# Rounding without a grid, two homes for rounded rows, and the last tiles in smaller parts

## What is computed

```python
x = x + L0_ffn(L0_cond(x, fside, ...))      # attention, then experts: silu(h @ w1) * (h @ w3) @ w2
x = x + L1_ffn(L1_cond(x, fside, ...))

def reorder_quantize(x, idx):               # L1_ffn
    scale = max(abs(x)) / (448 * 6)
    xr = (x / scale)[:, idx]
    scale_x = max(abs(xr), axis=1) / 448    # one for each row
    return fp8_e4m3(xr / scale_x), scale_x, scale
g = quantised(x) @ quantised(w_gate)        # 256 -> 704
u = quantised(x) @ quantised(w_up)
t = silu(g) * u
y = quantised(t) @ quantised(w_down)        # 704 -> 256
```

## Time and profile before

| | us |
|---|---|
| median of 3 runs | 626.72 (625.84 to 627.07) |
| profiled execution | 625.02 |
| its span | 623.2 |
| mean granted clock of TensorE | 0.961 |

### The profile page before, as it was taken

One profiled execution on the slowest core, in us unless ns is written; L12 is line 12 of the kernel. 1 busy time (PEld: TensorE's weight loads), 2 busy tenths in 40 slices (PEclk: granted clock), 3 DMA queues, 4 the chain that ended last, 5 costly groups with the idle time before them and its releaser, 6 DMA issues.

```text
span 623.2 us, 10889 instructions
## 1 busy us (share of the span) xinstructions
PE 495.9 (80%) x3862; PEld 406.4 (65%) x3862; DVE 506.2 (81%) x981; ACT 361.1 (58%) x762; POOL 241.2 (39%) x204
## 2 busy tenths in 40 slices
PE   2011298599999999999748999999999999475774
PEld 1000143278888878888618999999999999332542
DVE  4999878688888888987354979989999899489993
ACT  3336235777787778876307457565555556356671
POOL 3244014744444445541436079642514420170011
PEclk9999999989999999999859999999999999888897
DMA  8300004050000000000149799889888753130001
GB/s 267 135 1 1 0 1 135 0 178 2 1 2 2 1 2 9 19 9 2 58 157 357 259 331 281 273 267 257 300 290 271 274 130 119 34 103 17 9 25 36
DMA packets 36530, 71.87 MB, mean 115 GB/s; under 512 B 5275, under 2 KB 21915, under 8 KB 36219
## 3 DMA queue, kind: packets, MB, share of 16 engines
q10 hardware_dynamic: 15280, 40.77, 19.6%
q1 hardware_dynamic: 18123, 22.26, 10.6%
q0 software_dynamic: 3072, 8.14, 5.2%
HBM read 66.03 MB, written 5.12 MB: 114 GB/s over the span
## 4 chain that ended last, share of the span: by engine, by line
PE 55%; DVE 27%; issue 7%; ACT 5%; DMA 3%; POOL 1%; SPq 1%; DVEq 0%; ACTq 0%; POOLq 0%; PEldq 0%
PE pw L437 9%; PE pb L437 9%; PE pt L631 6%; PE pb L631 6%; PE sc L478 6%; PE sc L631 6%; PE po L437 5%; PE pt L489 3%; DVE areg L1181 2%; DVE areg L1167 2%; DVE areg L1165 2%; DVE rs L1579 2%; DMA wreg<-in_L_ffn_w 1%; DVE breg L1238 1%; DVE areg L1614 1%
## 5 line engine op out<-in xcount | busy, mean ns | idle before, releaser
L1730 POOL TENSOR_TENSOR breg<-breg,con 128x512 f32<-128x512 f32 x32 | 40.7, 1272 | 81.4 <-ACT breg L864 81.4
L437 PE MATMUL pb<-areg,wreg 128*128 128x512 f16 x240 | 58.4, 379 | 2.1 <-ACT breg L864 1.9
L437 PE MATMUL pw<-areg 128*128 128x256 f16 x406 | 56.5, 273 | 2.7 <-DVE areg L1533 2.7
L872 ACT ACTIVATE breg<-breg,mx 128x128 f32<-128x128 f32 (+1 forms) x128 | 56.5, 444 | 2.0 <-DVE mx L1289 2.0
L478 PE MATMUL sc<-areg,breg 128*128 128x128 f32 (+1 forms) x256 | 48.6, 334 | 6.7 <-DVE mx L1289 5.5
L631 PE MATMUL pb<-areg,wreg 128*128 128x128 f32 x448 | 52.7, 275 | 0.6 <-ACT areg L965 0.6
L985 ACT CAST areg<-areg 128x512 f16<-128x512 f32 (+1 forms) x46 | 25.9, 563 | 46.8 <-DVE areg L1519 43.6
L631 PEld LDWEIGHTS pb<-areg,wreg 128*128 128x128 f32 x448 | 51.3, 192 | 0.9 <-issue 0.8
L631 PE MATMUL pt<-areg,wreg 128*128 128x128 f32 x424 | 49.9, 275 | 1.3 <-DMA wreg<-in_L_ffn_w 1.3
L631 PEld LDWEIGHTS pt<-areg,wreg 128*128 128x128 f32 x424 | 48.5, 192 | 1.5 <-DMA wreg<-in_L_ffn_w 1.4
L631 PE MATMUL sc<-areg,wreg 128*128 128x128 f32 x416 | 48.9, 275 | 0.0
(11 more groups left out here) (250 smaller groups left out, 1286.4 us busy)
## 6 DMA issues: line engine op xcount, KB each, us to landing
wreg<-in_L_ffn_w ACTq DMA_DIRECT2D x40, 896.0 KB, 8.1
wreg<-in_L_ffn_w SPq DMA_DIRECT2D x14, 896.0 KB, 8.3
ys_dram<-areg ACTq DMA_DIRECT2D x23, 128.0 KB
wreg<-in_L_ffn_wq SPq DMA_DIRECT2D x1, 2048.0 KB, 8.9
wreg<-in_L_ffn_wo SPq DMA_DIRECT2D x1, 2048.0 KB, 8.2
areg<-in_fside_BxSxS ACTq DMA_DIRECT2D x4, 256.0 KB, 5.4
x_in<-in_x SPq DMA_DIRECT2D x4, 256.0 KB, 3.9
h_dram<-areg SPq DMA_DIRECT2D x8, 128.0 KB, 1.7
```

The lines of the kernel that those rows point to most:

```text
L437: last = nc.tensor.matmul(bank, w(a), m(b), start=first and k == 0, stop=final and k == 2)
L872: last = nc.scalar.activation(pr[:, parity, b, o:o + w], pr[:, parity, b, o:o + w], ACT.Exp, bias=mx[:, parity, k:k + 1], scale=-1.0, accu ...
L1730: G.tensor_tensor(t2[:, parity, :].rearrange("p (b n) -> p b n", b=2), t2[:, parity, :].rearrange("p (b n) -> p b n", b=2), rope_sin.rearr ...
```

## The change

In `nearest_e4m3` the instruction that takes the exponent bits goes. ScalarE makes the raised value with `Abs` instead of `Copy` and a factor of 2**20 - 2**10 instead of 2**20, and VectorE adds and takes off that value itself. `scale_of_rows` takes the reciprocal of the peak first. `qt` gets a second home. The last row tile (7) is scaled, rounded, transposed and copied in two halves of 352, with its down product in `sc2`, between other TensorE work in a new order. The w2 of the last expert tile (22) is split at the end of iteration 21; the folds of layer 2 move behind it. Lines of a part that repeat its pattern are left out.

```diff
+RAISE = 2.0 ** 20 - 2.0 ** 10
-        qt = cut(areg, 4864, INTER // 2, F16)
+        qts = [cut(areg, at, INTER // 2, F16) for at in (4864, 14464)]
...
 # TensorE
+            def part_transposes(i, h, bank):
+                pe.wait_ge(s["qt_ready"], i + 1 + h)
+                for c in range(h * NI // 2, (h + 1) * NI // 2):
+                    last = nc.tensor.transpose(bank[0:IQ, :].bitcast(F16)[:, c * P:(c + 1) * P], qts[i % 2][:, c * IQ:(c + 1) * IQ], identb[:, :])
+                last.then_inc(s["qtT_done"], 1)
+            def part_products(i, h):
+                pe.wait_ge(s["qtT_copied"], i + 1 + h)
+                for c in range(h * NI // 2, (h + 1) * NI // 2):
+                    last = nc.tensor.matmul(sc2[:, 1, 0:D], qtT[i % 2][0:IQ, c, :], q1d[0:IQ, c, :], start=c == 0, stop=c == NI - 1)
+                if h == 1:
+                    last.then_inc(s["dn_done"], 1)
...
             inner_transposes(NT - 2)
             down_quantised(NT - 3)
-            keep_clock(pt2[:, 1, :], 3)
+            pe.wait_ge(s["inner_ready"], NT)
+            keep_clock(pb[0], 4)
+            pe.wait_ge(s["qtT_copied"], NT - 1)
+            part_transposes(NT - 1, 0, pt2[:, 0, :])
+            part_transposes(NT - 1, 1, pt2[:, 1, :])
             down_quantised(NT - 2)
-            inner_transposes(NT - 1)
-            keep_clock(pt2[:, 1, :], 4)
-            down_quantised(NT - 1)
+            part_products(NT - 1, 0)
+            part_products(NT - 1, 1)
...
 # ScalarE, expert loop
-                if n < MT:
+                if n < MT - 1:
                     w2_high(n, parity)
                     inner_high(n, parity, 0)
+                if n < MT:
                     act.wait_ge(s["upb_done"], n + 1)
...
+                    if n == MT - 1:
+                        inner_high(n, parity, 0)
                     inner_high(n, parity, 1)
...
-                if n in (20, 21):
-                    fold_high(n - 20)
+                if n == MT - 2:
+                    w2_high(MT - 1, 1 - parity)
+                if n >= MT - 1:
+                    fold_high(n - MT + 1)
...
 # ScalarE, second layer (the same in scaled_input)
-                nc.scalar.activation(traised[i % 2], tvals[i % 2], ACT.Copy, scale=rs[:, 9, i:i + 1]).then_inc(s["scaled_ready"], 1)
+                nc.scalar.activation(traised[i % 2], tvals[i % 2], ACT.Abs, scale=rs[:, 9, i:i + 1]).then_inc(s["scaled_ready"], 1)
+            def scaled_parts(i):
+                act.wait_ge(s["inv_ready"], i + 1)
+                act.wait_ge(s["qt_ready"], i - 1)
+                for h in range(2):
+                    at = slice(h * IH, (h + 1) * IH)
+                    nc.scalar.activation(tscaled[i % 2][:, at], tvals[i % 2][:, at], ACT.Copy, scale=rs[:, 8, i:i + 1])
+                    nc.scalar.activation(traised[i % 2][:, at], tvals[i % 2][:, at], ACT.Abs, scale=rs[:, 9, i:i + 1]).then_inc(s["scaled_ready"], 1)
...
 # VectorE, expert loop
-                w2_low(n, n % 2)
+                if n < MT - 1:
+                    w2_low(n, n % 2)
                 inner_low(n, n % 2, 1)
...
-                if n >= MT - 2:
-                    fold_low(n - MT + 2)
+                if n == MT - 2:
+                    w2_low(MT - 1, (MT - 1) % 2)
+            for m in range(2):
+                fold_low(m)
...
 # VectorE, second layer
-                link(V.tensor_scalar(out, peak, 1.0 / FP8_MAX, None, ALU.mult))
-                link(V.reciprocal(inverse, out))
-                V.tensor_scalar(raised, inverse, 2.0 ** 20, None, ALU.mult).then_inc(done, 1)
+                link(V.reciprocal(turned, peak))
+                V.tensor_scalar(inverse, turned, FP8_MAX, None, ALU.mult)
+                V.tensor_scalar(raised, turned, FP8_MAX * RAISE, None, ALU.mult).then_inc(done, 1)
+                return V.tensor_scalar(out, peak, step, None, ALU.mult)
...
-                link(V.tensor_scalar(g.bitcast(I32), raised.bitcast(I32), 0x7F800000, 0x00400000, ALU.bitwise_and, ALU.bitwise_or))
-                link(V.scalar_tensor_tensor(v, g, FP8_LEAST * MAGIC, v, ALU.max, ALU.add))
-                return V.scalar_tensor_tensor(dst, g, FP8_LEAST * MAGIC, v, ALU.max, ALU.subtract, reverse1=True)
+                link(V.scalar_tensor_tensor(v, raised, FP8_LEAST * MAGIC, v, ALU.max, ALU.add))
+                return V.scalar_tensor_tensor(dst, raised, FP8_LEAST * MAGIC, v, ALU.max, ALU.subtract, reverse1=True)
...
             def round_inner(i):
                 dve.wait_ge(s["scaled_ready"], i + 1)
-                if i >= 1:
-                    dve.wait_ge(s["qtT_done"], i)
+                if i >= 2:
+                    dve.wait_ge(s["qtT_done"], i - 1)
...
-            round_inner(NT - 1)
+            round_parts(NT - 1)
```

More of the change, by code:

```diff
@@ L709, in inner_transposes @@
                 for c in range(NI):
-                    last = nc.tensor.transpose(pt2[0:IQ, 0, :].bitcast(F16)[:, c * P:(c + 1) * P], qt[:, c * IQ:(c + 1) * IQ], identb[:, :])
+                    last = nc.tensor.transpose(pt2[0:IQ, 0, :].bitcast(F16)[:, c * P:(c + 1) * P], qts[i % 2][:, c * IQ:(c + 1) * IQ], identb[:, :])
                 last.then_inc(s["qtT_done"], 1)
@@ L1055, in scaled_input @@
                     nc.scalar.activation(xval[:, k, :], xmix[:, i, :], ACT.Copy, scale=rs[:, 4, i:i + 1])
-                    last = nc.scalar.activation(xraised[:, k, :], xmix[:, i, :], ACT.Copy, scale=rs[:, 5, i:i + 1])
+                    last = nc.scalar.activation(xraised[:, k, :], xmix[:, i, :], ACT.Abs, scale=rs[:, 5, i:i + 1])
                 last.then_inc(s["xscaled_ready"], 1)
@@ L1073, in scaled_inner, with copy_parts @@
                 nc.scalar.activation(tscaled[i % 2], tvals[i % 2], ACT.Copy, scale=rs[:, 8, i:i + 1])
-                nc.scalar.activation(traised[i % 2], tvals[i % 2], ACT.Copy, scale=rs[:, 9, i:i + 1]).then_inc(s["scaled_ready"], 1)
+                nc.scalar.activation(traised[i % 2], tvals[i % 2], ACT.Abs, scale=rs[:, 9, i:i + 1]).then_inc(s["scaled_ready"], 1)
[6 more added lines that the diff above has]
+                    nc.scalar.activation(traised[i % 2][:, at], tvals[i % 2][:, at], ACT.Abs, scale=rs[:, 9, i:i + 1]).then_inc(s["scaled_ready"], 1)
+            def copy_parts(i):
+                act.wait_ge(s["dn_done"], i - 1)
+                for h in range(2):
+                    act.wait_ge(s["qtT_done"], i + 1 + h)
+                    nc.scalar.copy(qtT[i % 2][0:IQ, h * NI // 2:(h + 1) * NI // 2, :],
+                                   pt2[0:IQ, h, :].bitcast(F16)[:, h * NI // 2 * P:(h + 1) * NI // 2 * P].rearrange("p (c n) -> p c n", n=P)).then_inc(s["qtT_copied"], 1)
             def copy_qtT(i):
@@ L1107, in _ @@
             for j in range(2, NT):
-                if j + 1 < NT:
+                if j + 1 < NT - 1:
                     scaled_inner(j + 1)
+                elif j + 1 < NT:
+                    scaled_parts(j + 1)
                 if j + 2 < NT:
@@ L1113, in _ @@
                     copy_qxT(j + 3)
-                copy_qtT(j)
+                if j < NT - 1:
+                    copy_qtT(j)
+                else:
+                    copy_parts(j)
         @block.vector
@@ L1595, in mix_input @@
                 link(V.tensor_tensor(value, xsig[:, first:first + count, :], ratio1[:, first:first + count, :], ALU.mult))
-                scale_of_rows((2, 0, 4, 5), value, first, count, s["xinv_ready"])
-                V.tensor_scalar(rs[:, 3, first:first + count], rs[:, 0, first:first + count], 1.0 / WS, None, ALU.mult).then_inc(s["xout_ready"], 1)
+                scale_of_rows((2, 0, 3, 4, 5), value, first, count, s["xinv_ready"], 1.0 / (FP8_MAX * WS)).then_inc(s["xout_ready"], 1)
             def round_input(g):
@@ L1603, in round_input @@
                     dve.wait_ge(s["qxT_done"], first + count - 4)
[L1604 to L1605 removed]
+                nearest_e4m3(qx[:, first // 2 % 2, first % 2:first % 2 + count, :], xval[:, 0:count, :], xraised[:, 0:count, :]).then_inc(s["qx_ready"], 1)
             def inner_rows(i):
@@ L1630, in output_rows @@
                     dve.wait_ge(s_o[k], 16 * (i // 2))
-                V.scalar_tensor_tensor(yo[:, k, :], pw[:, 0:D], rs[:, 7, i:i + 1], srow[:, 2 * INTER:], ALU.mult, ALU.mult)\
+                V.scalar_tensor_tensor(yo[:, k, :], pw[:, 0:D] if i < NT - 1 else sc2[:, 1, 0:D], rs[:, 7, i:i + 1], srow[:, 2 * INTER:], ALU.mult, ALU.mult)\
                     .then_inc(s["yo_read"], 1)
```

20 lines of the change are left out of this document (13 added, 7 removed).

## The result

The changed kernel takes 619.30 us (618.26 to 620.54, 4 runs), the kernel before on the same chips 626.89 (625.84 to 629.23). The ratio is 0.9882, 95% interval 0.9858 to 0.9906: by the ratio 7.4 us less, with some 1.5 of uncertainty either way (the medians are 7.6 apart). Forecast were 617.8 and 8.9 less. The profiled execution is the slowest of the four: 620.54, span 618.6.

What follows compares the result with a forecast made beforehand. VectorE was taken to set the last expert tile's end and the row loop, ScalarE's chain close behind. Gains 1.55 + 1.47 + 1.6 + 0.8 + 3.5 = 8.9 us off 626.72 gave 617.8, range 615.0 to 620.8.

Steps and rivals of the forecast that it cites:

- Expert tile, 1.55: Last expert tile: with w2 split and folds moved behind, its last low half of the inner row ends 1.55 us earlier.
- The two fold_low and fold_high ... cost nothing.: Behind the last expert tile: moved folds fit VectorE's 8.01 us idle; without that cover they would cost 3.2.
- Grid removed: Rounding without the grid instruction and with shorter scale chains: 1.47 us in the head, 1.6 in tiles 2 to 4, 0.8 in the loop.
- The second chain: Row loop: ScalarE's scale, two scalings and next Silu hold a pass at 4.78 us, where VectorE alone needs 4.44.
- its dearer end: Each Abs on ScalarE might take 0.09 us more than the assumed 0.87, 0.7 over eight tiles.
- Tail, 3.5: From the last inner_rows: last output_rows at 8.85 us instead of 12.39, 3.5 less, if TensorE runs at 2.4 GHz.
- I take 2.4 GHz here: Tail: a gap of 3.3 us without wide matmuls leaves the clock high, as another of 3.2 did.
- My second figure: Tail at 1.2 GHz: last output_rows at 10.5 us, a gain of 1.9.
- Rival 3, table loads: Each Abs brings a table load of 1.28 us, and the next Silu or Sigmoid another: 633.2 us, chance 0.04.
- Rival 2, VectorE stays the bound: Row loop: passes of 4.44 us and 1.0 more off, 616.8; chance 0.04.
- Rival 4: Last expert tile gains nothing, a further 1.5 us standing in front of w2_high: 619.4; chance 0.05.
- Rival 1, the clocks: Head and tail gaps: clock both low 619.4 us, chance 0.20; both high 616.1, chance 0.18; head high, tail low 617.7.

Runs made afterwards that it cites:

- e1: The kernel before with the rounding alone (no grid instruction, Abs, shorter scale chain): 621.02 us, ratio 0.9893.
- e3: The kernel before with the two homes and the last row tile in halves alone, grid kept: 627.03 us, ratio 0.9980.
- e8: The kernel before with twelve more products of zeros in TensorE's last idle gap: 626.78 us, ratio 0.9980.
- e2: The kernel before with the new order of the last expert tile alone (w2 split, folds behind): 625.99 us, ratio 0.9974.
- e6: The changed kernel with w2_high of tile 22 ahead of inner_high(21, 1) and both folds one iteration earlier: 617.58 us, ratio 0.9832.
- e9: The changed kernel again with no edit, as reference: 619.12 us, ratio 0.9870 to the kernel before.
- e10: e4 with the last output rows in a buffer of their own: 616.71 us, ratio 0.9853 to the kernel before.
- e5: The changed kernel with ScalarE's Silu of tiles 5 to 7 ahead of the scalings of the tile before: 617.13 us, ratio 0.9836.
- e11: The changed kernel with eight more products of zeros behind the sixteen ahead of tile 2: 618.12 us, ratio 0.9870.
- e4: The changed kernel with ten more products of zeros behind down of tile 4, in TensorE's last gap: 617.28 us, ratio 0.9844.

## Why the prediction was right or wrong

The time (619.3) lies in the range of 615.0 to 620.8, the direction is right, and the gain is 7.4 where 8.9 was forecast. That the total came so near owes something to luck: in the profiled pair the tail gave 2.9 too little and the head 1.55 too much, each by a clock that went the other way. By its steps:

*Expert tile, 1.55.* Right by its mechanism. w2_high started at 530.40, 0.82 behind the start of the load of its number (529.58), as the exposed load had said, and VectorE waited 0.94 for it. 1.36 instead of 1.55: w2_low began 0.20 behind the end of w2_high, not 0.04. What I missed is beyond it: in the profiles with the shorter gap the clock stayed up, and where it fell (e1, e3, e8) down took 1.4 to 1.7 longer.

*"The two fold_low and fold_high ... cost nothing."* Wrong, and the largest fault of reasoning. VectorE was idle, but it isn't alone: the first gather took 0.85 longer beside the fold, and that gather is on the chain. I asked which engine waits, and not what else runs beside the moved instruction. e2 has the loss, e6 takes it away.

*Grid removed.* The head in the profile gave 3.02 instead of 1.47, since the clock this time stayed at 1.00; for that case 26.7 was worked out, and four profiles have 26.85 to 26.92. The 1.47 itself isn't shown, since at the low clock the head is a draw: 28.05 to 29.24 with the rounding of the change (e9, e6, e1, e10), 28.94 to 30.76 without it (e2, e8, the kernel before, e3). Tiles 2 to 4 gave 1.58 for 1.6, the loop 0.85 for 0.8, passes of 4.77 for 4.78. The second chain was the point of this part: the plain sum of removed instructions said 0.61 a pass, the trace gave 0.28, and e5 shows that the rest was waiting behind ScalarE's order. Abs took 0.87 in one pass and 0.86 in another, the time of Copy, so that term held and its dearer end was not needed.

*Tail, 3.5.* The step that failed is "I take 2.4 GHz here". The transposes of tile 6 came 4.15 behind the last inner_rows (4.17 worked out), but the clock had fallen 0.5 before them, so they were slow too, and the gap without wide matmuls became 3.7 (601.56 to 605.25) instead of 3.3. The gap of 3.3 was no protection either: in e9 it was 3.3 and the clock fell behind it. It fell in all five profiles that have this tail unfilled (the changed kernel, e5, e6, e9, e11), so one gap of 3.2 that had not lowered it was too little to choose 2.4 GHz by. My second figure, a gain of 1.9 with the last output_rows at 10.5, was too high for the profiled execution: I let the clock rise at 8.1, as before, and it rose at 10.5 (610.7), so down of tile 6 and the transposes ran slowly too. But it is what three of the five show (10.57, 10.48 and 10.47 in e5, e6 and e11), where the clock had risen before down of tile 6. e4 shows that the clock is the cause, 9.92 against 11.82, and e8 that it is new as a cause: before, down of tile 6 waited for output_rows of tile 5 anyway. At the high clock the last output_rows came at 9.92 and not 8.85: 0.5 of it is the write of tile 5 (e10), 0.4 the rounding of the first half beside POOL's addition, 0.93 instead of 0.52 (seen in each profile with this tail, and not tested by itself).

*Rival 3, table loads.* None came, 16 in the span before and after: between Abs and Silu the starts in the loop are 0.77 apart (593.81 to 594.58), with nothing between.
The Trainium skill (ScalarE: Activation LUTs, Table sets) says that abs is in every set, and this trace agrees.

*Rival 2, VectorE stays the bound*: refuted by e1 and made true by e5. *Rival 4*: not seen. *Rival 1, the clocks*: this is where the time went. The forecast's case (one high, one low) did occur, in the other order than I had it: head high, tail low. The prediction gave it the same time (617.7), with 1.9 for the tail; with the 0.57 that this profile shows it would have said 619.0.

So where are the 1.5? The parts behind w2_low of tile 21 gave 6.51 in the profiled pair where 8.9 was forecast: 0.2 in the expert tile, 0.9 at the gather and 2.9 in the tail are missing, and 1.55 in the head came on top. The runs' 7.4 lie between; that each execution draws its own clocks would explain it, and no run separates it.

## What to carry to other kernels

When an instruction leaves a full engine, look for the chain through the *other* engines that runs just behind: here 0.28 of 0.61 a pass was to be had before it became the bound, and a new order on ScalarE gave back the rest for nothing. "Hidden in idle time" holds only if nothing on the critical path is slowed by what is moved into that idle time. And when TensorE bounds a tail, try filling its last gaps: with ten products that nobody reads the tail took 9.92 (e4), and 10.47 to 11.82 in five profiles without them. Look then where the clock falls next (e8), and price a gap that can go either way as a chance, from several profiles.

## What the runs showed of the hardware

- The granted clock of TensorE differed between executions of one kernel and in the same gap. Idle times of 2.7 before the last down left it at 2.4 GHz in one execution and let it fall in three; the same tail took 11.82, 10.99, 10.57, 10.48 and 10.47, in the first with the clock low from 603.9 to 610.7 and in e11 from some 603.0 to 606.4; and in the changed kernel's profile it was 0.50 from 20 to 80 (mean 0.903). The effect looks like a microsecond or so, not clear of noise: of ten runs of the changed kernel the four with a mean clock of 0.90 took 618.26 to 620.75 (mean 620.1), the others 617.55 to 619.61 (618.8).
- A scalar_tensor_tensor on VectorE with both inputs in SBUF and POOL's work slow each other, and which of them pays differs. A gather's issue took 1.86 beside a fold that had started 0.64 earlier and 1.01 without, while the fold took 1.62 either way. A rounding of 352 values took 0.93 beside an addition on POOL and 0.52 without, one of 704 values 1.14 and 0.88 (e1), and the addition 0.93 beside the first and 0.72 alone. inner_rows, which has one input in PSUM, ran beside the same addition at 0.95 and the addition at 0.72.
